# Key pages handed to later steps, and row sums broadcast before the pages, in a fused LoRA, attention and dense kernel

## The reference

```python
x = x + L0(x)   # gated MLP, 1376 wide, with LoRA adapters
x = x + L1(x)   # attention, below
x = x + L2(x)   # quantised 512x512 weights and a LoRA delta
x = x + L3(x)   # one of eight 512x512 weights per sequence
```

```python
q = rope(rmsnorm(x @ Wq.T)); k = rope(rmsnorm(x @ Wk.T)); v = x @ Wv.T
kc = k_cache[block_table].reshape(bsz, L, HK, D)   # 16 pages of 32 keys
vc = v_cache[block_table].reshape(bsz, L, HK, D)
scores = einsum(q, concat([kc, k])) * SCALE        # 640 keys, masked by length
probs = softmax(scores); o = einsum(probs, concat([vc, v])); return o @ Wo.T
```

## Time and profile before

| | |
|---|---|
| median of 3 runs | 1372.97 us (1372.57 to 1373.29) |
| profiled execution | 1375.03 us, its span 1373.4 us |
| TensorE, VectorE, ScalarE, GpSimd busy | 99%, 74%, 71%, 55% of the span |
| chain that ended last | TensorE 94%, DMA 2%, ScalarE, VectorE, SyncE's queue and issue 1% each |
| granted TensorE clock | 1.00 |
| DMA engines busy | 0.7 to 0.8 of the first 230 us, 0.2 to 0.5 later |
| key pages | 128 DMAs of 128 KB, 3.7 us from issue to landing (median) |
| put and broadcast of row sums | 64 each; landing of the two together 1.4 to 5.5 us |

### The profile page before, as it was taken

One profiled execution on the slowest core, in us unless ns is written; L12 is line 12 of the kernel. 1 busy time (PEld: TensorE's weight loads), 2 busy tenths in 40 slices (PEclk: granted clock), 3 DMA queues, 4 the chain that ended last, 5 costly groups with the idle time before them and its releaser, 6 DMA issues.

```text
span 1373.4 us, 26359 instructions
## 1 busy us (share of the span) xinstructions
PE 1364.4 (99%) x7842; PEld 1188.1 (87%) x7842; DVE 1014.7 (74%) x2115; ACT 978.2 (71%) x1990; POOL 750.2 (55%) x990
## 2 busy tenths in 40 slices
PE   9999999999999999999999999999999999999998
PEld 7888878888888888888888888888888888888887
DVE  5887776777777777777777777777777777777776
ACT  5767665666777777777777777777777767777853
POOL 5421324666765576557655665666566656665600
DMA  7877889574424233424242324232424242433344
GB/s 196 261 260 222 279 271 297 128 177 120 96 63 109 66 98 70 113 64 96 66 108 63 93 62 108 62 93 62 108 62 94 62 108 63 94 67 67 86 156 153
DMA packets 256739, 165.80 MB, mean 121 GB/s; under 512 B 157413, under 2 KB 223846, under 8 KB 251094
## 3 DMA queue, kind: packets, MB, share of 16 engines
q1 hardware_dynamic: 249952, 142.48, 39.4%
q0 software_dynamic: 5376, 19.60, 5.3%
q10 hardware_dynamic: 1270, 2.04, 0.4%
HBM read 158.66 MB, written 38.94 MB: 144 GB/s over the span
## 4 chain that ended last, share of the span: by engine, by line
PE 94%; DMA 2%; ACT 1%; issue 1%; SPq 1%; DVE 1%; POOLq 0%; POOL 0%; ACTq 0%; DVEq 0%
PE proj_ps L1543 18%; PE sc L1580 16%; PE o_ps L1620 16%; PE ring L1598 10%; PE sc L1317 9%; PE proj_ps L1636 4%; PE proj_ps L1639 4%; PE proj_ps L1647 4%; PE proj_ps L1317 4%; PE o_ps L1317 3%; PE ring L1659 2%; PE ring L1409 1%; DMA inv_dram<-inv 1%; PE ring L1672 0%; PE proj_ps L1526 0%
## 5 line engine op out<-in xcount | busy, mean ns | idle before, releaser
L2233 DVE TENSOR_TENSOR pTl<-ring,pTh 128x512 fp32r<-128x512 f32 x320 | 215.3, 689 | 135.4 <-ACT pTh L1045 131.3
L1034 ACT ACTIVATE p_sb<-p_sb,bias,rstd 128x640 f32<-128x640 f32 x254 | 233.5, 920 | 50.6 <-DVE bias L2216 50.5
L746 POOL TENSOR_TENSOR rstd<-var,half_neg 128x4 f32<-128x4 f32 x64 | 65.1, 1016 | 297.3 <-DVE var L2265 297.3
L2200 DVE CUSTOM_DVE_ANT_0 p_sb<-sc,mask 128x640 f32<-128x640 f32 x254 | 204.4, 823 | 27.3 <-PE sc L1580 21.4
L1045 ACT ACTIVATE pTh<-ring 128x512 fp32r<-128x512 f32 x320 | 184.4, 599 | 27.1 <-PE ring L1598 25.5
L1598 PE MATMUL ring<-ident,p_sb 128*128 128x128 f32 x1270 | 180.7, 272 | 0.7 <-ACT p_late L1034 0.6
L1598 PEld LDWEIGHTS ring<-ident,p_sb 128*128 128x128 f32 x1270 | 151.8, 140 | 27.3 <-DVE pTl L2233 0.9
L1543 PE MATMUL proj_ps<-wh,xh 128*128 128x256 f32 (+1 forms) x484 | 169.1, 349 | 0.0
L1580 PE MATMUL sc<-kTh,qTh 128*128 128x320 f32 x512 | 162.7, 318 | 0.5 <-DVE kTl L2307 0.5
L1543 PE MATMUL proj_ps<-wl,xh 128*128 128x256 f32 (+1 forms) x484 | 161.8, 334 | 0.0
L1543 PE MATMUL proj_ps<-wh,xl 128*128 128x256 f32 (+1 forms) x484 | 161.4, 333 | 0.0
(11 more groups left out here) (281 smaller groups left out, 3635.9 us busy)
## 6 DMA issues: line engine op xcount, KB each, us to landing
v_pages<-in_v_cache POOLq DMA_DIRECT2D x128, 128.0 KB, 4.0
k_pages<-in_k_cache SPq DMA_DIRECT2D x128, 128.0 KB, 3.7
k_raw<-k_pages SPq DMA_DIRECT2D x256, 64.0 KB, 2.8
v_raw<-v_pages SPq DMA_DIRECT2D x64, 256.0 KB, 4.5
rope<-rope_dram SPq DMA_DIRECT2D x64, 256.0 KB, 4.0
inv_row<-inv_dram SPq DMA_DIRECT2D x64, 256.0 KB, 4.4
stage<-in_Wqkv SPq DMA_DIRECT2D x32, 384.0 KB, 5.1
w_raw<-in_WguT SPq DMA_DIRECT2D x19, 512.0 KB, 5.4
```

Of the source, the lines that this page charges most:

```text
L746: pool.tensor_tensor(rstd[:, u.k % 2, 0:REP], var[:, u.k % 2, 0:REP], half_neg[:, 0:REP], ALU.pow).then_inc(S["q_pow"], 1)
L1034: act_e.activation(weights_of(u, h), weights_of(u, h), ACT.Exp, bias=bias[:, h:h + 1], scale=rstd[:, u.k % 2, h:h + 1], accum_out=total[:, ...
L2200: v.tensor_tensor_reduce(out=weights_of(u, h).rearrange("p (s k) -> p s k", s=2), in0=score_ps[h % 2][:, :, 0:SPLIT], in1=mask[:, u.seq, : ...
L2233: v.tensor_tensor(pTl[:, c, :], ring[c % 2][:, :], pTh[:, c, :].bitcast(F32), ALU.subtract).then_inc(S["ptl"], 1)
```

## The change

Three edits.

1. SyncE: in every step the order is put, broadcast (with its wait for the put's landing), then two pages. The second batch of pages of a step is 2, 0, 4, 7, 7 and 6 in steps 0 to 5, where it was 2 and then 4 in each of the steps 1 to 6. By the running count the last batch has 4 pages left to issue, and none are left for step 6.
2. VectorE: the third unit's cached keys are turned ahead of the first unit's `invert`, in place of between its fourth and fifth `low_pt`; its `mean_square_k` changes places with `low_new_v`.
3. ScalarE: `high_cached_k(third)` goes ahead of the fourth `high_pt(first, ...)`, `lay_inv(first)` ahead of `exp(second, 0)`, and `scale_k(third)` ahead of `square_q(third)`.

```diff
+KEYS_AFTER = (2, 0, 4, 7, 7, 6)
@@ SyncE
             def step(u):
                 put_inv(u + -2)
-                if u.k == 2:
-                    spread_inv(u + -2)
+                spread_inv(u + -2)
+                if u.k < B - 1:
                     copy_keys(2)
-                else:
-                    if u.k < B - 1:
-                        copy_keys(2)
-                    spread_inv(u + -2)
                 if (u + -1).exists() and u.k > 1:
                     load_v(u + -1)
                 if (u + 1).exists():
@@
                     load_k(u + 1)
                 load_next_in(u)
                 load_next_out(u)
-                if u.k < B - 1:
-                    copy_keys(4 if u.k else 2)
+                if u.k < B - 2:
+                    copy_keys(KEYS_AFTER[u.k])
@@ ScalarE
             high_pt(first, 1)
             high_pt(first, 2)
+            high_cached_k(third)
             high_pt(first, 3)
             high_pt(first, 4)
+            lay_inv(first)
             exp(second, 0)
-            lay_inv(first)
-            high_cached_k(third)
+            scale_k(third)
             square_q(third)
-            scale_k(third)
             run_steps(step, 3, UNITS)
@@ VectorE
             low_new_k(second)
+            turn_cached_k(third)
             invert(first)
             low_x1(7)
             low_pt(first, 0)
@@
             low_pt(first, 3)
-            turn_cached_k(third)
             low_pt(first, 4)
+            mean_square_k(third)
             low_new_v(third)
-            mean_square_k(third)
             norm_o(first)
```

## The result

The changed kernel takes 1378.94 us (median of 6 runs, 1377.72 to 1379.43) against 1373.14 for the kernel before in the same runs: a ratio of 1.0039 with a 95% interval of 1.0029 to 1.0050. It is 5.8 us slower; forecast were 1378.5 and slower.

The account below looks back on a forecast made before the run. TensorE, busy 1364.4 of 1373.4 us, was taken as the bound, so only its pauses count: new ones of 1.3 and 6.0 less 1.87 gained give +5.5 on 1372.97, forecast 1378.5 us, range 1371.0 to 1383.5.

Parts of the forecast that it names:

- the deadline: Latest start of ScalarE's layout without a TensorE pause: 2.62 us before TensorE is ready for the output matmuls.
- The gain: TensorE's pauses in the third unit (1.25 us) and fourth unit (0.62) both go: 1.87 us saved.
- The queue's issue times: SyncE's in-order queue: 1.26 us per further page, 8.09 for seven; third unit's put 2.5 us late, fourth's 7.5.
- The landings: SyncE's transfers: a put right behind a page lands in 4.1 us, the first unit's put in 1.4, broadcasts in 3.9.
- step 3: SyncE's seven-page tail makes the third unit's put leave at 292.2, causing a new TensorE pause of 1.3 us.
- step 4: SyncE's seven-page tail and weight loads make the fourth unit's put leave at 314.9, causing a TensorE pause of 6.0 us.
- The order as a cost: SyncE issues nothing while waiting for a put's landing ahead of the pages: 2.9 us in step 3, 4.1 in step 4.
- The clock: Rival 2: TensorE comes out of the 6 us pause slow, adding 2.5 us, total 1381.0; chance 0.22.
- Step 5: The fifth unit's put causes no TensorE pause, since the stalls have given SyncE's queue its time back.
- Rival 1: SyncE's queue keeps up and only the gain is left: 1371.1 us; chance 0.12.
- Rival 3: First two units: the 1.25 us pause only falls to 0.6, late puts cost 1 to 2; about 1373; chance 0.09.
- Rival 4: SyncE's queue doesn't catch up in step 5; one more stall of 2 to 4 us, 1384; chance 0.07.

Follow-up runs that it names:

- table_only: Kernel before with only the second page batches changed to 2, 0, 4, 7, 7, 6, old order and no moves: 1379.35 us, ratio 1.0035.
- moves_only: Changed kernel with SyncE's order and page batches as before, so only the VectorE and ScalarE moves remain: 1374.19 us, ratio 0.9998.
- step4_short: Changed kernel with three pages moved from step 4 to step 5 (second batches 2, 0, 4, 7, 4, 7): 1376.92 us, ratio 1.0018.
- order_only: Kernel before with only the broadcast put ahead of the two pages in every step: 1373.40 us, ratio 0.9994.
- sevens_weights_later: Changed kernel with the second head's four weight slices loaded in step 6 in place of step 4, batches untouched: 1373.80 us, ratio 0.9996.
- busy_pause: Changed kernel with 16 needless matmuls on TensorE inside the pause of step 5: 1377.39 us, ratio 1.0025.

## Why the prediction was right, and where not

- **What bounds the kernel, and the deadline: right.** TensorE's pauses carry the whole difference, and 2.62 us from layout to output came out as 322.39 - 319.80 = 2.59.
- **The gain, 1.87: measured 1.59.** The first pause kept 0.28, the second went whole. The credit for the first was partly wrong. I gave it to the moves on ScalarE and VectorE and to the early put; table_only has the pause gone (0.07) without any move, and moves_only has it longer. It was the pages in front of the first put. The prediction also says that k_cos no longer stands behind the inverse's layout. It still does: in the changed order the layout and an exponential come right before `scale_k(third)`.
- **The queue's issue times: right.** Seven pages took 8.17 and 8.10 us (8.09 forecast), weights 2.12 (2.45), key loads 2.59 and 2.97 (3.0). The third unit's put left at 291.80 (292.2), the fourth's at 313.21 (314.9), 7.2 us late (7.5). But that pages never vary was a misreading: in before two other batches of four took 4.72 and 4.70 us, and seven took 9.20 in step4_short.
- **The landings: mis-sized.** Behind a page a put took 3.15 and 2.53 us, to the broadcasts of 294.95 and 315.74; I took 4.1 from puts that had landed in 3.75 and 4.4. The broadcasts took 3.5 and 4.0 (3.9). That is the main term by which step 3 made no pause (1.3 forecast) and step 4 one of 4.5 (6.0). The first unit's put erred the other way: it landed in 2.9 us and not 1.4, so its broadcast left at 261.01 (259.95), 2.2 us earlier than in before and not 3.3.
- **The order as a cost: wrong in part.** I charged the wait in front of the pages to the queue. It is there in the queue's time, but order_only shows no loss, and table_only has nearly the same loss without it: its broadcasts, issued right behind two pages, landed in 4.8 and 5.2 us, those of after in 3.5 and 4.0.
- **The clock: priced right, given too small a chance.** I made it a rival with 0.22 and +2.5 us; it happened, at 2.7. The forecast's number was met because a pause 2.8 us too long made up for a clock that it left out. The mechanism of the prediction is the measured one, and the agreement of 1378.5 with 1378.9 is partly luck.
- **Step 5: right.** The stalls gave the queue its time back: the put of the fifth unit left right behind its reciprocal in after.
- **The other rivals: out.** Rival 1 needed a put at most 4.7 us late, and it was 7.2. Rival 3 had 0.6 us of the first pause kept and the late puts at 1 to 2; they were 0.28, and 4.5 with a slow clock behind. Rival 4 needed one more stall, and the seventh unit has none.
- **The rule on DMA issue** (in the Trainium skill's "DMA: Bandwidth & Descriptors", that initiating is usually small beside the transfer) gave no warning here: a page holds this queue for 1.26 us against 3.7 from issue to landing, and seven in a row, 8.1 us, hold it longer than any put or broadcast took to land.

## What to carry to other kernels

When a queue's work is moved, add up the issue times of each period with everything that stands in it, waits too, and compare them with the period; the step that was already full (here the one with the weights) decides, not the average. Then follow the one small transfer at the end of that queue to the engine that sets the end: here 2 KB of row sums, not the megabytes of pages. And give a pause of several microseconds on TensorE a second price, the half clock behind it.

## What the runs showed of the hardware

- TensorE's granted clock was 0.50 from the end of a pause of 4.5 us for 6.4 us (after), 0.50 from 324 to 327 us behind one of 5.0 (table_only), and 0.61 on average over 3.6 us behind one of 3.4 (step4_short). It stayed 1.00 through a pause of 1.5 (sevens_weights_later) and through 5.9 us of which needless matmuls filled 3.8 (busy_pause). The prices were 2.7, 1.6 and 1.5 us, so the longest pause had not the highest.
- Issuing a 128 KB page whose number is read from memory holds SyncE's queue for 1.26 us in most cases. Over all runs four in a row took 4.29 to 5.07 us, and seven 8.10 to 8.17 with one of 9.20. Four key loads of 64 KB took anything from 1.9 to 4.3 us.
- From 250 to 400 us a broadcast issued right behind two page copies, with a value load behind it, landed in 4.5 to 5.2 us (11 cases, in before, moves_only and table_only). With the put in front and page copies behind it landed in 3.0 to 4.6 (44 cases in all runs), and with the put in front and a value load behind in 3.4 to 4.7 (53 cases). So the long landings go with the pages in front and not, as the prediction read them, with the values behind. No run changed this by itself.
